# Adding a constant to minus the row maximum on VectorE instead of as a bias of ScalarE's exponentials

## The reference

```python
Q = (x @ Wq.T + bq).reshape(B, N, H, HD)      # H = 16, HD = 64, N = 2048
K = (x @ Wk.T + bk).reshape(B, N, H, HD)
V = (x @ Wv.T + bv).reshape(B, N, H, HD)
scores = jnp.einsum('bnhd,bmhd->bhnm', Q, K)
scores = scores * (SCALE * adaptive_scale)[None, :, None, None] / TEMP
w = jax.nn.softmax(scores, axis=-1)
attn = jnp.einsum('bhnm,bmhd->bnhd', w, V).reshape(B, N, H * HD)
```

## Time and profile before

| what | value |
|---|---|
| time, median of 3 runs | 2480.86 us (2479.13 to 2484.33) |
| time of the profiled execution | 2484.54 us |
| its span, first to last instruction | 2482.7 us |
| mean granted TensorE clock | 0.974 of full speed |
| PE busy | 2204.1 us, 89% of the span |
| DVE busy | 1730.8 us, 70% |
| ACT busy | 1714.3 us, 69% |
| POOL busy | 1435.3 us, 58% |
| L450 POOL, low parts, x512 | 1096.4 us |
| L634 and L636 ACT, exponentials, x512 each | 569.7 us and 566.3 us |

### The profile page before, as it was taken

One profiled execution on the slowest core, in us unless ns is written; L12 is line 12 of the kernel. 1 busy time (PEld: TensorE's weight loads), 2 busy tenths in 40 slices (PEclk: granted clock), 3 DMA queues, 4 the chain that ended last, 5 costly groups with the idle time before them and its releaser, 6 DMA issues.

```text
span 2482.7 us, 47718 instructions
## 1 busy us (share of the span) xinstructions
PE 2204.1 (89%) x17317; PEld 1696.9 (68%) x17317; DVE 1730.8 (70%) x3019; ACT 1714.3 (69%) x2160; POOL 1435.3 (58%) x794
## 2 busy tenths in 40 slices
PE   5889889898888988888889989867999999999998
PEld 3666666666666666666666666645788887788786
DVE  6777777777778677677687777676666665666652
ACT  3888888788788788788788888822545544545554
POOL 5787787787788778778778778812312311312300
PEclk7999999999999999999999999987999999999999
DMA  4000000000000000000000000010000000000000
GB/s 98 1 1 1 1 1 2 2 2 1 2 1 1 2 1 1 2 1 2 2 1 1 1 1 1 1 43 1 1 1 1 1 1 2 1 1 1 1 1 17
DMA packets 15276, 13.06 MB, mean 5 GB/s; under 512 B 3120, under 2 KB 14384, under 8 KB 14768
## 3 DMA queue, kind: packets, MB, share of 16 engines
q1 hardware_dynamic: 15024, 9.72, 1.4%
HBM read 8.67 MB, written 1.05 MB: 4 GB/s over the span
## 4 chain that ended last, share of the span: by engine, by line
issue 35%; PE 34%; POOL 16%; DVE 11%; ACT 3%; POOLq 0%; SPq 0%; DMA 0%; DVEq 0%; ACTq 0%
POOL PAB L450 11%; PE RING L1215 5%; PE ST L1319 4%; PE OO L1458 3%; PE ST L1320 3%; PE OO L1269 3%; DVE maxes L874 3%; POOL F L510 2%; POOL QL L434 2%; PE OO L1270 1%; PE RING L1411 1%; PE RING L1195 1%; PE RING L1236 1%; PE ST L1481 1%; PE RING L1391 1%
## 5 line engine op out<-in xcount | busy, mean ns | idle before, releaser
L450 POOL TENSOR_TENSOR PAB<-PR,PAB 128x1024 f16<-128x1024 f32 x512 | 1096.4, 2144 | 327.7 <-ACT PAB L636 309.8
L874 DVE TENSOR_REDUCE maxes<-RING 128x1 f32<-128x512 f32 (+1 forms) x1344 | 879.6, 670 | 349.1 <-PE RING L1215 228.1
L634 ACT ACTIVATE PR<-ST,lift 128x1024 f32<-128x1024 f32 x512 | 569.7, 1113 | 279.8 <-PE ST L1320 240.2
L636 ACT ACTIVATE PAB<-ST,lift 128x1024 f16<-128x1024 f32 x512 | 566.3, 1106 | 0.0
L1215 PE MATMUL RING<-KH,QL 128*128 128x512 f32 x1024 | 459.3, 455 | 103.9 <-DVE maxes L874 97.1
L1269 PE MATMUL OO<-VP,PAB 128*128 128x130 f16 x4096 | 497.4, 224 | 12.2 <-POOL PAB L450 11.0
L1319 PE MATMUL ST<-QL,KH 128*128 128x512 f32 x1024 | 452.8, 442 | 50.3 <-DVE QH L886 32.7
L1269 PEld LDWEIGHTS OO<-VP,PAB 128*128 128x128 f16 x4096 | 361.2, 98 | 196.0 <-issue 127.0
L1270 PE MATMUL OO<-VP,PAB 128*128 128x66 f16 x4096 | 463.3, 193 | 0.0
L1320 PE MATMUL ST<-QH,KL 128*128 128x512 f32 x1024 | 405.0, 396 | 0.0
L1270 PEld LDWEIGHTS OO<-VP,PAB 128*128 128x128 f16 x4096 | 370.5, 99 | 11.0 <-issue 10.0
(11 more groups left out here) (141 smaller groups left out, 2958.7 us busy)
## 6 DMA issues: line engine op xcount, KB each, us to landing
X<-in_L_attn_a_x SPq DMA_DIRECT2D x4, 256.0 KB, 3.5
SHARED<-in_rope_cos SPq DMA_DIRECT2D x1, 1024.0 KB, 4.8
SHARED<-in_rope_sin SPq DMA_DIRECT2D x1, 1024.0 KB, 7.0
out<-X SPq DMA_DIRECT2D x4, 256.0 KB, 2.3
RAW<-in_L_attn_a_Wq SPq DMA_DIRECT2D x1, 512.0 KB, 7.0
RAW<-in_L_attn_a_Wk SPq DMA_DIRECT2D x1, 512.0 KB, 8.2
RAW<-in_L_attn_a_Wv SPq DMA_DIRECT2D x1, 512.0 KB, 6.3
RAW<-in_L_attn_a_Wo SPq DMA_DIRECT2D x1, 512.0 KB, 7.2
```

Of the source, the lines that this page charges most:

```text
L450: pool.tensor_tensor(PB[:, s, :], PR[:, step % 2, :], PA[:, s, :], ALU.subtract).then_inc(p_low_pool, 1)
L634: act.activation(PR[:, step % 2, :], ST[step % 2][:, :], ACT.Exp, bias=lift[:, :])
L636: act.activation(PA[:, step % SLOTS_A, :], ST[step % 2][:, :], ACT.Exp, bias=lift[:, :]).then_inc(sa.exps, 1)
L874: dve.reduce_max(maxes[:, qt, c:c + 1], bank[:, 0:width], X_AXIS).then_inc(s.ring_taken, 1)
```

## The change

The constant moves. `lift` and its memset go away. Both exponentials of the first attention are issued without a bias. In `take_max` the CAST of L878 becomes a `tensor_scalar` that adds the constant `lifted` and rounds, and the subtraction of L879 becomes a `scalar_tensor_tensor` that computes (negmax + lifted) - first half. `lifted` is log 256 in the first attention and 0 in the second, so the second attention gets the new kinds of instruction too, 32 times each. No instruction changes its place in any engine's order, and no wait is added or removed; VectorE has one memset fewer.

```diff
-LIFT = 2.0 ** 8
+LIFT_A = float(np.log(2.0 ** 8))
...
-        lift = sb("lift", [P, 1])
...
-                        act.activation(PR[:, step % 2, :], ST[step % 2][:, :], ACT.Exp, bias=lift[:, :])
+                        act.activation(PR[:, step % 2, :], ST[step % 2][:, :], ACT.Exp)
                         wait(act, sa.pv, g - SLOTS_A + 1)
-                        act.activation(PA[:, step % SLOTS_A, :], ST[step % 2][:, :], ACT.Exp, bias=lift[:, :]
+                        act.activation(PA[:, step % SLOTS_A, :], ST[step % 2][:, :], ACT.Exp
                                        ).then_inc(sa.exps, 1)
...
-            dve.memset(lift[:, :], float(np.log(LIFT)))
...
-            def take_max(s, bank, item, qt, c, width, chunks, last):
+            def take_max(s, bank, item, qt, c, width, chunks, last, lifted=0.0):
...
                     link(dve.tensor_reduce(negmax[:, :], maxes[:, :, 0:chunks], X_AXIS, ALU.max, negate=True))
-                    link(dve.tensor_copy(negparts[:, 0:BT].bitcast(F32R), negmax[:, :]))
-                    dve.tensor_tensor(negparts[:, BT:AUX], negmax[:, :], negparts[:, 0:BT],
-                                      ALU.subtract).then_inc(s.max_ready, 1)
+                    link(dve.tensor_scalar(negparts[:, 0:BT].bitcast(F32R), negmax[:, :], lifted, None, ALU.add))
+                    dve.scalar_tensor_tensor(negparts[:, BT:AUX], negmax[:, :], lifted, negparts[:, 0:BT],
+                                             ALU.add, ALU.subtract).then_inc(s.max_ready, 1)
...
-                take_max(sa, RING[n % 2], n, i // 4, i % 4, BLK, BLOCKS, i == 15)
+                take_max(sa, RING[n % 2], n, i // 4, i % 4, BLK, BLOCKS, i == 15, LIFT_A)
...
-                                take_max(sa, bank, n, j // 4, j % 4, BLK, BLOCKS, j == 15)
+                                take_max(sa, bank, n, j // 4, j % 4, BLK, BLOCKS, j == 15, LIFT_A)
```

## The result

| kernel | median, us | runs | ratio to before, 95% interval |
|---|---|---|---|
| before | 2481.21 | 6 (2479.13 to 2484.33) | |
| changed | 2617.70 | 6 (2600.05 to 2624.89) | 1.0541 (1.0507 to 1.0576) |

Slower by 5.4%, 136 us, where I forecast 1.7%. The time lies outside my range. The profiled execution took 2622.61 us. The second attention is unchanged. The first attention, from GpSimd's first L449 to its last, took 1550.9 us before (63.2 to 1614.1) and 1686.7 us after (63.2 to 1749.9), 135.8 us more: all but 2 us of the difference between the two profiled executions.

The account below looks back on a forecast made before the run. Four engines near their limit, none setting the time everywhere, ScalarE on the path only in places. Projection units +28.5, query block 3 +22.8, pairs elsewhere -8.3 made +43.0 us: 2524 us, slower by 1.7%, range 2482 to 2545.

Parts of the forecast that it names:

- -8.3: Pairs of exponentials on the path outside projection units: 46 places gain 0.18 us each, -8.3 us.
- +51.3: New blocks of VectorE's second `negparts` instruction behind GpSimd: +28.5 us in projection units and +22.8 us in query block 3.
- 76 places: 47 VectorE waits for a high part plus about half of TensorE's 58 for a low part; at 0.18 us, 13.7 us.
- all 105 waits: Upper bound on the gain: every VectorE wait for a high part and TensorE wait for a low part counts, 19 us.
- Projection units, +28.5: GpSimd's pause before L450 closes, shutting out the second `negparts` instruction: 30 units at 0.95 us, 28.5 us slower.
- Query block 3, +22.8: GpSimd starts 0.18 us earlier, so the second `negparts` instruction is blocked in 12 of 15 units at 1.9 us.
- Values units, 0: Eight are already blocked; in the other seven the second instruction would end shortly before L857 is due: no cost.
- New kinds, 0: VectorE's `tensor_scalar` and `scalar_tensor_tensor` on four columns take the times of the instructions they replace: no cost.
- Only the projection units: First rival: 0.04 us is not enough to block in query block 3; +20.2 us, 2501 us; chance 0.30 with its variant.
- No new blocks, faster: Rival: VectorE's second `negparts` instruction still gets through, so the exponentials' gain gives -13.7 us, 2467 us; chance 0.13.
- No faster: Rival: the exponentials get no faster because a default bias is read all the same; 2481 us; chance 0.04.
- My sign for the blocks: In the profile after, the second `negparts` instruction's group has 50 blocks instead of 8, about 110 us instead of 30.6.

Follow-up runs that it names:

- with both waits: GpSimd waits at step 6 for VectorE's `negparts` instructions and at step 2 for its division: added to the changed kernel 0.9852 (2452.6 us), to the kernel before 0.9937 (2472.5 us).
- with the division's alone: Changed kernel plus only GpSimd's wait at step 2 of a unit, until VectorE's division has ended: 1.0237 of the kernel before, 2546.1 us.
- the kernel with one shorter exponential: Changed kernel with a zero bias column put back on the second exponential (L635) only: 1.0099 of the kernel before.
- the kernel that waits for `negparts` alone: Changed kernel plus only GpSimd's wait at step 6 of a unit, until VectorE has finished `negparts` for the next unit: 1.0361 of the kernel before.
- filling the pauses: 20 unread matmuls at step 3 added to the changed kernel with only the `negparts` wait: 1.0138 of the kernel before, 2522.5 us, against 1.0361; output not the reference's.
- the first three experiments: Changed kernel, zero bias column on both exponentials: 1.0000; kernel before, only bias column removed: 1.0535; changed kernel, zero column on second exponential: 1.0099.

## Why the prediction was wrong

The runs split the 5.41%, at 24.8 us for 1%. How much of a term is clock is an estimate: its difference in time at the lower level by the 0.40 above. The time at that level in the first attention was 28.6 us before, 14.7 us there with both waits; in the changed kernel 20.5 us with both waits, 96.9 us with the division's alone, 198.5 us without.

| from, to | measured | of it clock | my term |
|---|---|---|---|
| before, with both waits: 8 old blocks gone | -16 | -6 | |
| exponentials shorter | -21 | +2 | -8.3 |
| `negparts` blocked again, 56 times | +96 | 31 | +51.3 |
| 18 divisions passed over twice | +75 | 41 | 0 |
| sum | +134 | 68 | +43.0 |

The split depends on the order. Here the blocks of `negparts` are priced with no division passed over. Taken out of the changed kernel first, they gave 45 us, since the divisions that are passed over then rose from 18 to 30.

**What bounds the kernel; the exponentials.** Right. Each lost 90 to 93 ns, ScalarE's busy time fell by 95 us, the second of a pair starts 0.92 us after the first, and with four busy engines only a part of it reached the time. The gain on the path was probably undersized: 21 us, 15 to 26 by the scatter, where 76 places at 0.18 us gave 13.7 and all 105 waits would give 19. Whether pairs that show no such wait were on the path as well is open.

**Projection units, +28.5.** Right in number, 30 of 30, and near in price: the kernel with one shorter exponential, which has 30 such blocks and only 10 us more at the lower clock, lost 25 us. Wrong in which of the two instructions stands still, and that is not free. My working had the next scores 1.56 us behind the end of the second L449. Over the 30 units the median is 1.46 us where the second instruction stands (one shorter exponential) and 1.86 us where the first does (changed kernel): some 0.3 us a unit above my price, 9 us in all by this estimate.

**Query block 3, +22.8.** Twelve of fifteen, starting just behind L449, as forecast. No run isolates what they cost the kernel; from the first instruction to the next scores the median goes from 1.69 to 3.61 us, the 1.9 us of my price. All blocks of `negparts` together cost 96 - 16 = 80 us beyond the eight old ones. Less the clock's part of both (31 - 6) that is 55 us, against my 51.3, with some 5 us of scatter in it. So the two terms were mis-sized mainly by the clock.

**Values units, 0.** Six of the seven I called free were blocked too. Their price is inside the 55 us and was not isolated.

**New kinds, 0.** Right: 1.0000. One reading beside it was wrong: 1.13 us is the whole length of L878 in a values unit; against its 0.17 us it is 0.96 us too long. Nothing in the sum used it.

**The step that failed** is the list of places: "I read all 63 hand-overs in the timeline". I asked who slips through GpSimd's pauses at `negparts` and at no other instruction. The division was in the same position, on the same 0.19 us, and the profile said so before: its durations in the 63 units were 0.76 to 0.90 us (16), 1.34 to 1.36 (30) and 2.18 to 2.26 (17), three values for one shape, a sign that it stood still behind another engine. The 30 in the middle are the ones that could be passed over: the same 30 are, in the kernel that waits for `negparts` alone. My sum has no term for the division; it cost 75 us.

**The second failed step** is a term left out: TensorE's clock. I priced each pause at its length. The changed kernel has some 170 us more at 1.2 GHz, about 68 us of the 134 by the price above. For the kernel with the waits it was shown by filling the pauses; for the changed one it is carried over from there.

**The rivals.** "Only the projection units" is what the kernel with one shorter exponential does, 1.0% slower. "No new blocks, faster" is what both waits make true, 1.5% faster. Neither was this kernel. "No faster" fell with the groups of L633 and L635. My sign for the blocks, 110 us in the group of the second instruction, failed by its number: the group has 65.8 us, 26 blocks, less than the 87 us I had given the first rival, because the other 30 fell on the first instruction.

## What to carry to other kernels

When an engine gets faster, list every instruction of the other engines that gets in through one of its pauses, not only the one you have in mind: sort an engine's instructions of one shape by duration, and start with those that have two or three distinct durations. If a short instruction is on the path and a longer one that is not shuts it out, let the long one wait for it: here two such waits turned 5.4% slower into 1.5% faster. And price a pause of TensorE by what follows it as well: look whether matmuls of one shape take 0.40 or 0.63 us behind it.

## What the runs showed of the hardware

- A waiting VectorE instruction does not always get in when GpSimd's instruction ends. In the changed kernel it stood through the rest of one L449 and all of the next in 30 units at `negparts` (2.42 us for 128x4) and in 18 at the division (3.45 us). What decides this is open. In all 186 such cases of the runs, the exponential that the next low part reads had ended 0.23 to 0.42 us before GpSimd's instruction did. At other boundaries without a pause VectorE did get in: mostly with less than 0.22 us or with 0.59 to 0.88 us, but at one division of each of seven kernels with 0.30 to 0.37 us, inside the range of those passed over. So that distance alone does not settle it, and no run tested it.
- The order of starts decides at hundredths. Over five kernels (before, changed, and the first three experiments) every second instruction on `negparts` that started at least 0.02 us behind a GpSimd low part stood for over 2 us, and every one that started at least 0.02 us ahead took 0.16 us; no start lies in between. The Trainium skill, "SBUF — State Buffer", section "Who interferes with whom", has whichever starts first hold the ports for its whole instruction; the traces agree.
- TensorE's granted clock often falls to 1.2 GHz behind a pause, not always: within 5 us of the start of 18 of 18 pauses of 2.8 us in the changed kernel and of 25 of 30 in the one that waits for `negparts` alone, and behind 18 of the 30 double pauses of about 1 + 1 us in projection units. Each microsecond at that level cost 0.40 us here, and 640 matmuls that compute nothing gave back 2.2% of the time.
